# Extra matrix products that nobody reads, in the first stages of a fused transformer layer

## The reference

```python
x = x + attn(layernorm(x), W_qkv, b_qkv, W_out, b_out, rel_emb_k, rel_emb_v)
# attn: q, k, v = heads of x @ W_qkv + b_qkv ; q = q / sqrt(8)
#   dist = clip(j - i, -64, 64) + 64
#   score = q @ k.T + q . rel_emb_k[dist]
#   ctx = softmax(score) @ v + sum over j of attn * rel_emb_v[dist]
#   out = ctx @ W_out + b_out
x = x + memory_update(ctx_1024, layernorm(x), conv_w, conv_b)
x = x + block(layernorm(x))   # rotary attention, then shared and routed experts
```

## Time and profile before

| | |
|---|---|
| time, median of 3 runs | 457.0 us (451.66, 457.00, 460.88) |
| profiled execution: its own time | 448.09 us |
| its span, first to last instruction | 446.3 us |
| mean granted clock of TensorE in it | 0.917 |
| PE busy | 376.7 us (84%) |
| DVE, ACT, POOL busy | 286.7, 241.6, 150.2 us |

### The profile page before, as it was taken

The page is one execution under the profiler, slowest core; times in us unless marked ns, Lnnn a source line. Parts: engine busy times, 40 slices in busy tenths (PEclk is TensorE's granted clock), DMA queues, the critical chain, the costliest instruction groups (busy, mean ns, idle before and its releaser), DMA issues.

```text
span 446.3 us, 12142 instructions
## 1 busy us (share of the span) xinstructions
PE 376.7 (84%) x5006; PEld 194.6 (44%) x5006; DVE 286.7 (64%) x585; ACT 241.6 (54%) x500; POOL 150.2 (34%) x269
## 2 busy tenths in 40 slices
PE   1759878888898989888776889999999988889993
PEld 0312434566676667666643442222222222744541
DVE  5657463667777776760255576868999961645785
ACT  1536466676767666677300142688888885462110
POOL 6331063456766566575631108300000000300222
PEclk9955566999999999999999695999999999999998
DMA  7300000000000000000131001900000000000000
GB/s 242 99 0 20 4 1 5 4 9 18 7 4 6 4 7 6 5 5 5 60 100 46 1 0 51 221 11 2 2 1 2 0 3 1 1 0 0 7 18 24
DMA packets 12845, 11.18 MB, mean 25 GB/s; under 512 B 4535, under 2 KB 11111, under 8 KB 12663
## 3 DMA queue, kind: packets, MB, share of 16 engines
q1 hardware_dynamic: 11863, 7.27, 5.7%
q0 software_dynamic: 928, 3.15, 3.0%
HBM read 7.50 MB, written 2.10 MB: 22 GB/s over the span
## 4 chain that ended last, share of the span: by engine, by line
PE 66%; ACT 11%; DVE 9%; issue 6%; POOL 5%; DMA 2%; SPq 1%; POOLq 0%; ACTq 0%; DVEq 0%
PE ps L1312 7%; PE ps L1097 7%; PE ps L1126 6%; PE ps L1363 6%; PE ps L1299 5%; PE ps L1045 4%; ACT arena L573 4%; PE ps L1109 4%; PE ps L1144 4%; PE ps L1283 4%; PE ps L1067 3%; PE ps L1253 2%; PE ps L988 2%; PE ps L1291 2%; ACT arena L647 2%
## 5 line engine op out<-in xcount | busy, mean ns | idle before, releaser
L750 DVE TENSOR_REDUCE m_qk<-ps 128x2 f32<-128x1024 f32 x64 | 76.9, 1223 | 33.2 <-PE ps L1067 33.1
L877 DVE TENSOR_REDUCE m_qk<-ps 128x2 f32<-128x1024 f32 x64 | 75.2, 1218 | 14.7 <-PE ps L1283 14.5
L573 ACT ACTIVATE arena<-ps 128x512 f32<-128x512 f32 x128 | 69.6, 597 | 21.7 <-PE ps L1109 20.6
L647 ACT ACTIVATE arena<-ps 128x512 f32<-128x512 f32 x128 | 66.9, 593 | 14.4 <-PE ps L1299 14.4
L405 POOL TENSOR_TENSOR rstd<-var,power 128x1 f32<-128x1 f32 (+1 forms) x28 | 17.4, 631 | 139.5 <-DVE var L797 126.9
L473 POOL TENSOR_TENSOR arena<-arena,eb 128x256 f32<-128x256 f32 x64 | 46.9, 733 | 51.0 <-ACT eb L561 28.4
L561 ACT ACTIVATE eb<-ps 128x512 f32<-128x512 f32 (+1 forms) x64 | 31.3, 541 | 28.3 <-PE ps L1097 28.3
L1299 PE MATMUL ps<-q_op,k_op 50*128 50x512 bf16 x128 | 35.2, 381 | 5.4 <-ACT arena L647 4.4
L474 POOL TENSOR_TENSOR arena<-arena,eb 128x192 f32<-128x192 f32 x64 | 38.3, 599 | 0.0
L1126 PE MATMUL ps<-arena,v_sb 128*20 128x128 f32 x1024 | 35.9, 283 | 1.3 <-POOL arena L474 1.3
L1109 PE MATMUL ps<-q_op,k_op 62*128 62x128 bf16 x512 | 26.6, 224 | 12.1 <-ACT arena L573 10.7
(11 more groups left out here) (199 smaller groups left out, 538.5 us busy)
## 6 DMA issues: line engine op xcount, KB each, us to landing
rel_v<-in_relv_ext SPq DMA_DIRECT2D x1, 1024.0 KB, 8.0
eb<-in_w SPq DMA_DIRECT2D x2, 512.0 KB, 6.2
scr<-part POOLq DMA_DIRECT2D x2, 384.0 KB, 3.5
q_op<-scr POOLq DMA_DIRECT2D x2, 384.0 KB, 7.3
k_op<-scr POOLq DMA_DIRECT2D x2, 384.0 KB, 8.5
x_sb<-in_x SPq DMA_DIRECT2D x2, 256.0 KB, 3.3
q_op<-farT SPq DMA_DIRECT2D x32, 3.0 KB
q_op<-farT SPq DMA_DIRECT2D x32, 1.5 KB
```

The source lines that it names most:

```text
L573: act.activation(p_ring[:, k % SLOTS_P, e, :], ps[:, bank, :], ACT.Exp).then_inc(sm["bank_free"], 1)
L647: act.activation(p_ring[:, v % RING, e, :], ps[:, bank, :], ACT.Exp).then_inc(sm["ring_free"], 1)
L750: dve.tensor_reduce(m_qk[:, u, n:H:PAIRS], ps[:, banks, :], AX_X, ALU.max).then_inc(sm["pair_free"], 1)
L877: dve.tensor_reduce(m_qk[:, IT * b + it, 2 * p:2 * p + 2], ps[:, 2 * (su % 2):2 * (su % 2) + 2, :], AX_X, ALU.max).then_inc(sm["rmax_done" ...
```

## The change

Products that nobody reads are added on PE at four places. Nothing is removed and no other engine's stream changes. PE's wait for `ld_sel` moves ahead of the transposes.

```diff
             pe.wait_ge(sm["ld_id"], 16)
+            for _ in range(12):
+                pe.matmul(ps[:, 2, 0:P], ident[:, :], ident[:, :], start=True, stop=True)
+            pe.wait_ge(sm["ld_sel"], 16)
             for b in range(B):
                 for tt in range(IT * b, IT * b + IT):
                     pe.wait_ge(sm["ln_out"], tt + 1)
                     pe.transpose(ps[:, b, (tt % IT) * P:(tt % IT) * P + P], xn[:, tt, :], ident[:, :]).then_inc(sm["xT_psum"], 1)
+                    busy(2, 1)
...
                 if kind == "pick":
                     of_k, two = picks_of(n)
+                    into = [bank_of(kind, u, n, k) for k in range(2)]
+                    busy(into[0], (8 if n == 0 else 3) if u == 0 else 2)
                     pe.wait_ge(sm["split_done"], 2 * u + of_k + 1)
-                    into = [bank_of(kind, u, n, k) for k in range(2)]
...
                         pe.wait_ge(sm["split_done"], (2, 4, 4)[n])
                     if u == 0 and n == 1:
                         pe.wait_ge(sm["vf_ready"], 1)
+                    if u == 0:
+                        busy(banks.start, 2)
                     for j in range(nh):
```

## The result

The changed kernel takes 459.8 us (median of 22 runs, 451.8 to 468.1), the kernel before 454.0 (22 runs, 445.5 to 460.9): a ratio of 1.014, 95% interval 1.009 to 1.020. All ratios here are taken over the executions within 1.5% of the shortest of their own kernel, the medians over all of them. The changed kernel is slower by 1.4%; 455 us and a small gain were forecast. The figures are from the first unless said.

A forecast was written before the change was run, and what follows sets the result against it. TensorE, 66% of the chain, was taken to bound the kernel through its low clock; -1.6 + 1.9 - 1.8 - 1.5 + 1.1 = -1.9 us, ratio 0.9958 on the 457.0 median, gave 455 us, range 444 to 464.

The forecast's parts named there:

- (a): Opening up to VectorE's split: added products raise the clock by 10 us, projections run high; -1.6 us, bounds +2.3 and -1.9.
- (b): Turns 1 to 7 and tile 0's classes, 25.12 to 39.60 us: products cost more than the high clock gives; +1.9 us.
- (c): 39.6 to 57.1 us, batch 1's turns 0 to 3: two thirds of the all-high gain; -1.8 us, bounds +3.9 and -2.7.
- (d): 57.1 to 78.4 us, batch 1's turns 4 and 5: two thirds of 2.2 us net; -1.5 us, bounds +1.9 and -2.2.
- (e): Batch 1's turns 6 and 7, at 86 and 95 us: clock already high, each pays two products; +1.1 us, firm.
- The rest: Everything behind batch 1's turn 7: as before, clock state entering later low stretches put at nothing, bounds -3 and +3 us.
- Rival 1: Whole kernel: high clock worth more in ordinary runs, 444 us in all runs, up to 448 with part; chance 0.22.
- Rival 2: Products do nothing for the clock outside their own turns, gain and price cancel: 458 to 459 us; 0.22 with a late-opening rival.
- Rival 3: Clock falls in the gap before turn 1 and stays down while products run: 466 to 473 us; chance 0.11.
- The terms all high: Case with the high clock held throughout the forecast's stretches: -3.7 us in sum, thus 453 us.

The follow-up runs named there:

- e7: The changed kernel once more, unaltered, for a second profile; ratio 1.013 to the kernel before.
- e6: The changed kernel with four unread products in place of two in each of batch 1's turns; ratio 1.023 to the kernel before.
- e2: The changed kernel without the two unread products in each turn of batch 1; ratio 0.988 to the kernel before.
- e13: The changed kernel with 24 single products, one before each maxima pair of tiles 0 to 2, replacing the two in each batch 1 turn; ratio 0.987 to the kernel before.
- e12: The kernel before with only the three products in batch 0's turns 1 to 7 and the two in tile 0's class steps; ratio 1.008 to the kernel before.
- e14: The kernel before with the opening's products and 24 single ones before maxima pairs, none in batch 0's later turns or class steps; ratio 0.997 to the kernel before.
- e4: The changed kernel with the products of turns 1 to 7, batch 1's turns and class steps on 32 of 128 columns; ratio 1.001 to the kernel before.
- e5: The kernel before with only GpSimd's output bias addition moved from the opening to behind the first tile's outer classes; ratio 0.996 to the kernel before.
- e8: The kernel before with the opening's products alone and GpSimd's output bias addition moved behind the first tile's outer classes; ratio 0.998 to the kernel before.

## Why the prediction was wrong, by its own steps

- **(a), the opening, -1.6 forecast, -3.4 measured.** Sign and mechanism right: first projections at the high level, ScalarE's first copy from 14.9 us. The clock's part is 1.2 in the two first profiles and 1.5 on average, close to the forecast; missed was the contest of VectorE's casts and GpSimd's addition, which turned out the other way in the changed kernel, 2.2 us. The twelve ended at 11.25 us, the late end of the range given; transposes and products then went at 0.33 us a tile, and the projections began at 13.95 and not at the 13.2 of the forecast, 0.35 us of it because the normalization itself began later (8.47 against 8.12).
- **(b), turns 1 to 7, +1.9 forecast, +1.7 measured,** with three products at 0.75 to 0.82 us and turns at 0.75 (0.78 and 0.82 forecast). Also right that turns 1 and 2 lose most: 3.1 us (21.7 to 24.8) in place of 1.48.
- **(c), -1.8 forecast, +2.8 measured: the step that failed.** "I take two thirds" of the gain of an all-high stretch was put on a balance of two stretches that had one product beside each pair of maxima, 0.7 to 3.8 us apart; the new pairs come 3.7 to 5.0 us apart in (c) and 11 to 14 in (d). The pattern was called the same and isn't. In its place the runs show a clock that falls at 41 to 43 us with two or four products a turn (changed, e7, e6) and is low for 38 to 44 us, no better than with none (e2, 38), so that the whole price is lost: 7 us between e2 and the changed kernel. That the number was not the point is shown by e6; that another placing holds the clock longer, by e13; why is open. With the clock low a pair costs 1.01 us; the bound of +3.9 held.
- **(d), -1.5 forecast, and (e), +1.1.** The same failure: both +4.4 against -0.4. (e) was right: its two pairs cost 0.59 each. That leaves +3.2 for (d), outside its bound of +1.9: its two pairs cost 1.01 each as the bound has it, but the bound kept the kernel before's clock, and 6.8 us at the high level that this had between 58 and 78 us were missing.
- **The rest,** forecast at nothing within 3 us. In the profiles 6 to 11 us come behind the context, mostly the long low stretch; in the medians, 1.4% against 0.9% at the context, some 2 us. This remains open.
- **The rivals.** Rival 1 is refuted: no execution of the changed kernel was under 451.8 us. Rival 2, "products do nothing for the clock outside their own turns", names what happened to the clock. That its 458 to 459 us lie near 459.8 is luck: it forecast +1.4 us on 457.0, and measured are +5.8 on 454.0, since it put the price of (c) and (d) at nothing. Rival 3's mechanism (low at turn 1) did not come; its place was 17 us later. e12 shows it by itself, without the opening: turn 7 ends 5.7 us late.
- **The range** held the time (459.8 in 444 to 464), the direction was wrong. That the forecast of 455 is only 4.8 us off is in part luck too: the 457.0 that it was put on, a median of three, was 454.0 over 22 executions, and its ratio of 0.9958 would have given 452.1. The terms all high add up to -3.5 and not to -3.7, which changes nothing.

## What to carry to other kernels

An unread product is paid wherever the engine is in the chain, here 0.2 to 0.3 us high and 0.5 low each; put it where a wait covers it or where it warms up a long run of heavy products (the opening: 1.1 to 1.7% faster alone), and not into a chain in which other engines' copies stand between the products. If a high level is to be held, try single products in many steps (e13, 14 us low) before bunches (e6, 44 us low), start from a high clock, since on a low one the same products did nothing (e14), and compute first what the high clock gives back in that stretch: here about what it cost. When the chain's products are followed by another engine's copies, halving their time gives little.

## What the runs showed of the hardware that was not expected

- The clock printed for the first microseconds can't be relied on: it is 1.00 up to 16.9 us in the kernel before, while weight loads 0.85 us apart become 0.43 apart there; the first clock record of that trace is at 17.0 us.
- Products of 128 rows on 32 columns kept TensorE at the high level as those on 128 columns did (e4, 1.00 from 24 to 38 us), while 4.73 busy us of 5 with 32 and 48 rows stood at 0.50.
- Casts on VectorE and an addition on GpSimd draw each other out, and who waits went with their starts in 15 of 15 profiles: with the addition 0.1 to 0.9 us behind the first cast, second cast 2.56 and addition 2.52 us (3); with both within 0.02 us, casts 0.41 each and addition 4.16 (12). It isn't a rule for every instruction: in e5 and e8 a smaller GpSimd step that began 0.1 us behind the first cast was itself drawn out, to 2.1 us.
